# The seams of a spectral tower and its tail: conjugate spectra, loads ahead of barriers, 64 x 64 tiles in self attention, experts in double steps

## The chip, the core and the metric

The program runs on one core of one Trainium2 chip. The core has five engines with queues of their own: TensorE (PE in the rows; its weight loads are PEld), VectorE (DVE), ScalarE (ACT), GpSimd (POOL) and SyncE (SP), which here only issues DMAs. The engines meet at semaphores. The metric is device time in microseconds from the first to the last instruction of a run. Everything is computed in float32. In the rows one matmul of the program is two MATMUL entries, so "x4" under TensorE is two matmuls.

## What is computed

The kernel computes a vision tower (a spectral network of four layers with a head), and then two blocks of attention and mixture of experts on the tokens that it gives. Cut to what matters:

```
h = einsum('bhwi,ic->bhwc', x, fc0_w) + fc0_b                  # x: 64 images of 64 x 64 x 3, 64 channels
for l in range(4):
    xf = rfft2(h)                                              # 32 x 16 modes are kept
    of[top] = einsum('bixy,ioxy->boxy', xf[top], w1)           # a complex 64 x 64 product for each mode
    of[bot] = einsum('bixy,ioxy->boxy', xf[bot], w2)
    y = irfft2(of) + pw_w[l] @ h + pw_b[l]
    h = gelu(batchnorm(y))                                     # over all images and pixels
tok = gelu(h @ fc1_w + fc1_b) @ fc2_w + fc2_b                  # 4096 tokens of 64
h = tok
h = h + linear_attention(layernorm(h))                         # 4 heads of 32, softmax over q and over k
h = h + experts(layernorm(h))                                  # 8 experts, 64 -> 256 -> 64, top 2
h = h + self_attention(layernorm(h))                           # over the 64 rows of each image, masked rows
h = h + experts(layernorm(h))                                  # 16 experts, 64 -> 128 -> 64, top 2
```

## The kernel before

**Phases.** The tower is a row of phases. At the end of each, `phase_end` (L162) drains every engine and waits for all five. First comes `spectrum0`; then, for each of the four layers l, `mix` (the products of the modes) and `inverse` (the inverse transforms, the pointwise product, the sums for batch norm); after the inverse of layers 0 to 2 comes `forward` (batch norm, gelu and the forward transform of that layer's result), after the inverse of layer 3 the `head`. The tail has no barriers inside; there semaphores between engines order everything. All phases share one SBUF area, `arena`, and address it by offset. So a phase can load ahead of a barrier only into parts that the phase before has finished with.

**mix** (L305 to L392). The modes come in NCH = 8 chunks in three sets of buffers. SyncE loads a chunk of spectra (`spec_in`, 2 MB) and of weights (2 MB). The complex product is made as a real one of 128 rows: `s_sb[:, 0]` holds the real parts on the lower 64 partitions and the imaginary ones on the upper 64. `s_sb[:, 1]` is made from it by two copies: ScalarE copies the imaginary part up (L368), VectorE the real part down (L378), and then VectorE negates the imaginary part in place (L380, it waits for L368). TensorE (L356) waits for all three. A chunk's result is made in two parts v; each is turned by VectorE (L391) and stored to `spec_out` by SyncE (L321, 1 MB). The last thing SyncE does before the barrier is to wait until these stores have landed (L340).

**inverse** (L417 to L641). It goes over NP = 32 pairs of images p. The column transform `rows(p)` (L490) takes its operand from `grp`, the spectra of eight images, loaded by SyncE from `spec_out` in four DMAs of four modes for each group (L439). VectorE turns its result (L592) into the stationary operand `a2`. `columns(p, T)` (L514) multiplies that with `hin`, in which one half of the partitions holds a constant basis and the other the activations. The basis of `hin[0]` and of `hin[1]` is written by VectorE at the start of each inverse (`fill_basis`, L469, two copies each); TensorE's first `rows` waits for the first two. In layers 1 to 3 the activations come from `y_dram` in two halves (L445) through a gelu on ScalarE (L548); in layer 0 from the input, after VectorE has cleared four areas (L606). ScalarE takes the result out of PSUM (L557) and stores it to `y_dram` (L561, 2 MB for each p). VectorE gathers the sums for batch norm (L600). GpSimd writes the pointwise weights of the second `a2` (L474). At the end VectorE aggregates 32 x 8 sets of sums in one instruction (L621); a chain of small instructions follows on VectorE and TensorE, ScalarE takes the root (L577), but only once its stores have landed, and VectorE makes `scale` and `shift` (L634 to L638).

**forward and head.** Both begin with loads of `y_dram` (L665, L796, 2 MB each) into four buffers `hf`, which SyncE issues after the barrier, and with gelus of them on ScalarE (L733, L839).

**The tail** has TG = 8 groups of 512 tokens. `vector_norm` (L975) is nine VectorE instructions over all tokens with one root on ScalarE. TensorE then turns the normed tokens (L1050), and computes on. In `tensor_attention` TensorE's order for step n is project(n), context(n-1), attend(n-1), turn_k(n), project_out(n-1), turn_q(n). In `tensor_self` (L1560 to L1619) it is project(n) (q: L1568, v: L1570, k: L1571), turn_prob(n-1) (L1586), scores(n) (L1577), mix(n-1) (L1596), project_out(n-1) (L1603). Which part of the array a matmul uses follows from its shape: "64*64" in a row is 64 rows of the array by 64 columns, "128*64" all rows by 64 columns. In `tensor_experts` each of NST = 64 steps is a `hidden` (L1451, two matmuls of 512 columns, one on each half of the array's rows), a relu by ScalarE for even steps (L1507) and by VectorE for odd ones (L1542), and a `second` (L1460, two matmuls, one on each half of the array's columns). It runs in the order hidden(i), second(i-2). Once in eight steps come `bias` (L1466) and `turn_y` (L1474). VectorE also scales the inputs of the experts (L1523).

## Time and profile before

| | us |
|---|---|
| median of 3 runs | 4860.54 (4859.98 to 4867.24) |
| the profiled execution | 4854.42 |
| its span, first to last instruction | 4852.6 |

| engine | busy, us | share of the span |
|---|---|---|
| TensorE, matmuls | 3665.2 | 76% |
| VectorE | 2948.8 | 61% |
| ScalarE | 2495.9 | 51% |
| GpSimd | 55.2 | 1% |

The granted TensorE clock has a mean of 0.895 of 2.4 GHz. All times in the rows below are microseconds from the start of the span of that one execution. No single engine bounds the program: it is a row of stages, each with a limit of its own, and gaps between them.

### The profile page before, as it was taken

The page shows a single profiled execution, that of the slowest core. Times are in us where ns is not written, and L with a number is a line of the kernel's source. Part 1 is how long each engine was busy: PE and PEld are TensorE (multiplying, and loading weights), DVE is VectorE, ACT ScalarE, POOL GpSimd, SP SyncE. Part 2 cuts the span into 40 slices and gives each one's busy share as a digit, 9 for nine tenths or more (in the row PEclk, how much of TensorE's full clock was granted, in tenths as well). Part 3 has the DMA queues.
Part 4 walks back from the last instruction along what each step waited for, and adds up shares of the span by engine and source line. Part 5 has one row for each costly group of instructions (what it writes and reads, how often), then busy time and mean ns, then how long its engine had stood idle before and what let it go on. Part 6 is the DMA issues. An engine that isn't in the chain of part 4 may idle for free. (4 is left out here: it accounts for less than half of the span.)

```text
span 4852.6 us, 114628 instructions
## 1 busy us (share of the span) xinstructions
PE 3665.2 (76%) x50692; PEld 2490.2 (51%) x50692; DVE 2948.8 (61%) x3816; ACT 2495.9 (51%) x1895; POOL 55.2 (1%) x56
## 2 busy tenths in 40 slices
PE   5796995669777746687877566878886998669777
PEld 4475883447566634475666344656663222642432
DVE  1458997874677768845777688457773000543345
ACT  0112444432488854324889543248887998222221
POOL 0000000000000000000000000000000001000000
PEclk9898997889899978898999788989999999779578
DMA  1675776759688867596898676868886542011042
GB/s 36 246 296 181 253 254 247 291 213 362 237 336 340 324 245 287 221 354 241 337 340 331 247 275 227 334 245 334 331 334 236 201 176 99 1 36 36 1 88 62
DMA packets 213395, 1119.87 MB, mean 231 GB/s; under 512 B 24593, under 2 KB 96561, under 8 KB 138989
## 3 DMA queue, kind: packets, MB, share of 16 engines
q1 hardware_dynamic: 189390, 827.97, 46.7%
q10 hardware_dynamic: 22592, 285.22, 15.5%
q8 instruction: 297, 4.87, 0.4%
q0 software_dynamic: 1024, 1.05, 0.1%
q14 instruction: 92, 0.75, 0.0%
HBM read 709.04 MB, written 405.14 MB: 230 GB/s over the span
## 5 line engine op out<-in xcount | busy, mean ns | idle before, releaser
L514 PE MATMUL bank<-arena 128*64 128x128 f32 x16384 | 1137.5, 295 | 206.9 <-ACT arena L557 187.9
L514 PEld LDWEIGHTS bank<-arena 128*64 128x64 f32 x16384 | 1080.3, 221 | 360.0 <-issue 359.8
L548 ACT ACTIVATE arena<-arena,shift,scale 64x2048 f32<-64x2048 f32 x384 | 804.1, 2094 | 130.8 <-DMA arena<-y_dram 89.5
L600 DVE BATCH_NORM_STATS2 stats<-arena 128x6 f32<-128x512 f32 x1024 | 633.3, 671 | 299.6 <-ACT arena L557 299.5
L592 DVE STREAM_TRANSPOSE arena<-bank 64x512 f32<-64x512 f32 x1024 | 731.2, 714 | 68.5 <-PE bank L490 37.1
L557 ACT ACTIVATE arena<-bank,pwb 128x1024 f32<-128x1024 f32 x512 | 567.2, 1108 | 290.1 <-PE bank L514 282.3
L356 PE MATMUL bank<-arena 128*32 128x128 f32 x8192 | 589.7, 475 | 95.6 <-DVE arena L380 95.6
L733 ACT ACTIVATE arena<-arena,shift,scale 128x1024 f32<-128x1024 f32 x384 | 445.1, 1230 | 404.9 <-DMA arena<-y_dram 404.9
L693 PE MATMUL bank<-arena,fwq 32*32 32x512 f32 x6144 | 310.5, 825 | 354.6 <-DVE arena L739 354.6
L356 PEld LDWEIGHTS bank<-arena 128*32 128x32 f32 x8192 | 464.1, 134 | 221.0 <-issue 97.7
L739 DVE STREAM_TRANSPOSE arena<-arena 128x1024 f32<-128x1024 f32 x384 | 447.4, 1203 | 37.5 <-ACT arena L733 37.5
L490 PE MATMUL bank<-arena,ga 64*64 64x512 f32 x2048 | 288.8, 684 | 179.6 <-DMA arena<-spec_out 117.3
L710 PE MATMUL bank<-arena,ghq 32*32 32x256 f32 x12288 | 351.8, 426 | 20.6 <-issue 16.1
L368 ACT ACTIVATE arena<-arena 64x4096 f32<-64x4096 f32 x32 | 127.1, 3972 | 466.4 <-DMA arena<-spec_in 466.4
L693 PEld LDWEIGHTS bank<-arena,fwq 32*32 32x32 f32 x6144 | 98.0, 116 | 475.7 <-issue 466.6
L710 PEld LDWEIGHTS bank<-arena,ghq 32*32 32x32 f32 x12288 | 282.6, 111 | 108.0 <-issue 77.9
L391 DVE STREAM_TRANSPOSE arena<-bank 128x512 f32<-128x512 f32 x256 | 160.7, 687 | 287.2 <-PE bank L356 287.1
L744 DVE STREAM_TRANSPOSE arena<-bank 128x1024 f32<-128x1024 f32 x192 | 235.6, 1229 | 115.8 <-PE bank L693 115.8
L810 PE MATMUL bank<-arena,fc 64*128 64x512 f32 x1024 | 264.4, 624 | 14.6 <-ACT arena L839 13.1
L846 ACT ACTIVATE arena<-bank,fc1b 128x1024 f32<-128x1024 f32 x256 | 267.9, 1124 | 13.6 <-PE bank L810 13.6
L864 DVE TENSOR_SCALAR arena<-bank,fc2b 128x512 f32<-128x512 f32 x8 | 6.0, 752 | 404.8 <-PE bank L822 404.8
L490 PEld LDWEIGHTS bank<-arena,ga 64*64 64x64 f32 x2048 | 76.9, 145 | 285.3 <-issue 275.7
(195 smaller groups left out, 2537.6 us busy)
## 6 DMA issues: line engine op xcount, KB each, us to landing
y_dram<-arena ACTq DMA_DIRECT2D x128, 2048.0 KB, 7.9
arena<-y_dram SPq DMA_DIRECT2D x128, 2048.0 KB, 8.7
arena<-y_dram SPq DMA_DIRECT2D x192, 1024.0 KB, 7.3
arena<-spec_in SPq DMA_DIRECT2D x32, 2048.0 KB, 7.9
arena<-in_w_modes SPq DMA_DIRECT2D x32, 2048.0 KB, 13.8
spec_out<-arena SPq DMA_DIRECT2D x64, 1024.0 KB, 15.6
arena<-spec_out SPq DMA_DIRECT2D x128, 512.0 KB, 9.3
spec_in<-arena SPq DMA_DIRECT2D x24, 2048.0 KB, 13.9
```

Source lines behind the costliest of these rows:

```text
L356: mm = pe.matmul(bank[4 * v + k // 4][t * HB:(t + 1) * HB, k % 4 * 2 * B:(k % 4 + 1) * 2 * B], w_sb[u][:, mode, t // 2 * HB:(t // 2 + 1) * ...
L490: mm = pe.matmul(bank[2 * v + r][FREQ[par], :], ga[k_p, r * S:(r + 1) * S], grp[p // Q % 2][k_p, :, par * Q + q, :], start=True, stop=True ...
L514: mm = pe.matmul(hpx(bank[4 + T % 2 * 2 + j // 4][CHAN[par], :])[:, :, j % 4 * S:(j % 4 + 1) * S], a2[p % 2][par][:, :, rp], hpx(hin[u][pa ...
L548: act.activation(hpx(hin[u][par][CHAN[par]])[:, :, px], yin[v][CHAN[par]], ACT.Gelu, bias=shift[CHAN[par], :], scale=scale[CHAN[par], :]). ...
L557: act.activation(y, banks[:, 4 + T % 2 * 2:6 + T % 2 * 2, :].rearrange("p b (h x) -> p b h x", h=2), ACT.Identity, bias=pwb[:]).then_inc(y ...
L592: dve.transpose(a2[p % 2][par][FREQ[par], v * 32 + c0:v * 32 + c0 + 16, :], banks[FREQ[par], 2 * v:2 * v + 2, :].rearrange("p r (k c) -> p ...
L600: dve.bn_stats(stats[:, p * 48 + 6 * t:p * 48 + 6 * t + 6], by_half(yout[p % 2])[:, T // 2, h, T % 2 * BK:T % 2 * BK + BK]).then_inc(y_see ...
L693: mm = pe.matmul(bank[g][QUAD[c], :], fwq[QUAD[g], s * 32:(s + 1) * 32], hT[q % 2][QUAD[g], s, :, c * CQ:(c + 1) * CQ], start=(s == 0), st ...
L710: mm = pe.matmul(bank[4 + c][QUAD[j], 0:256], ghq[QUAD[c], col:col + K1], t1[q % 2][QUAD[c], v:4:2, hh, :, ri * M2:(ri + 1) * M2], start=( ...
L733: act.activation(x, x, ACT.Gelu, bias=shift[:], scale=scale[:]).then_inc(f_ready, 1)
L739: dve.transpose(hT[p % 2][:, :, row:row + 16, :].rearrange("p s h c -> p h s c"), hf[p % Q][:, v * 2 * BK:(v + 1) * 2 * BK].rearrange("p ( ...
L846: act.activation(gb[n % NB_G], banks[:, 2 * k:2 * k + 2, :].rearrange("p a b -> p (a b)"), ACT.Gelu, bias=fc1b[:]).then_inc(fc1_gelu, 1)
```

## The change

It has two parts. **In the tower:**
- The constants of both forward transforms are changed so that the stored spectrum is the complex conjugate. The imaginary half of the operand then already has the sign that L380 gave it. ScalarE's copy gets a factor of -1 and VectorE's negation goes.
- In mix, after the stores of chunk 6, SyncE waits until they have landed, then loads 14 of the 16 modes of the inverse's first group, and, in layers 1 to 3, both halves of the first pair's activations. Only then come the stores of the last chunk. The last two modes are loaded after the barrier. `yin`, `yout` and `hin` change places in the arena, so that these loads meet nothing that is in use.
- At the end of the inverse SyncE loads the first two of forward's or head's four buffers ahead of the barrier, once the columns of pair 30 are done.
- One of the four basis copies moves from VectorE to GpSimd, in front of GpSimd's two old copies; TensorE's first `rows` waits for it as for VectorE's.
- The aggregation for batch norm is made in four parts of eight pairs, three of them inside the loop; the end then combines four means and variances, with more small instructions.

**In the tail:**
- `vector_norm` works on two halves of the tokens, in the order centre(0), variance(0), centre(1), scale(0), variance(1), scale(1). The turns on TensorE wait for the first half only, and for the second from the fifth group on.
- In the linear attention project(n+1) runs ahead, between turn_k(n) and project_out(n-1); VectorE masks the context before it shifts the exponents.
- In self attention project(n+1) moves behind mix(n-1). q and k become two column tiles that read the same rows, v and the output projection are cut from four matmuls of 128 columns of the array to eight of 64. VectorE sums the exponents right after the shift, ahead of add_out.
- The experts run hidden(i), hidden(i+1), second(i-2), second(i-1).

```
-    part = np.stack([np.stack([cs, -sn], 1), np.stack([sn, cs], 1)], 0)
+    part = np.stack([np.stack([cs, sn], 1), np.stack([sn, -cs], 1)], 0)
...
+            def ahead():
+
+                for u in range(2):
+                    sp.wait_ge(mixed_stored[u], l * (NCH * 16) + (NCH * 16 + 32 - 32 * u))
+                    sp.sem_inc(waited[sp.engine], 1)
+                load_group(sp, l, 0, slice(0, M2 - 2))
+                if not first:
+                    for v in range(2):
+                        load_half(sp, l, 0, v)
 
...
+                if c == NCH - 2:
+                    ahead()
...
-                pe.wait_ge(imag_negated, n + 1)
...
-                act.activation(s_sb[u][0:C, 1], s_sb[u][C:P, 0], ACT.Copy).then_inc(imag_up, 1)
+                act.activation(s_sb[u][0:C, 1], s_sb[u][C:P, 0], ACT.Copy, scale=-1.0).then_inc(imag_up, 1)
...
                 dve.tensor_copy(s_sb[u][C:P, 1], s_sb[u][0:C, 0]).then_inc(real_down, 1)
-                dve.wait_ge(imag_up, l * NCH + (c + 1))
-                dve.tensor_scalar(s_sb[u][C:P, 0], s_sb[u][C:P, 0], -1.0, None, ALU.mult).then_inc(imag_negated, 1)
...
-        hin = [[at((2 * u + par) * PX, PX) for par in range(2)] for u in range(2)]
-        yout = [at((4 + u) * PX, PX) for u in range(2)]
-        yin = [at(6 * PX + v * PX // 2, 2, PX // 4) for v in range(2)]
+        hin = [[at((3 * u + par) * PX, PX) for par in range(2)] for u in range(2)]
+        yin = [at(2 * PX + v * PX // 2, 2, PX // 4) for v in range(2)]
+        yout = [at((5 + u) * PX, PX) for u in range(2)]
...
-            for i in range(Q):
-                load_group(0, i)
...
-                    load_group(p // Q + 1, p % Q)
...
+            sp.wait_ge(y_done, (l * NP + NP) * 4 + 4)
+            sp.sem_inc(waited[sp.engine], 1)
+            for q in range(2):
+                sp.dma_start(hf[q], y_dram[q]).then_inc(f_loaded[q], 16)
...
+            pool.tensor_copy(basis_of(0, 1), basis_from(1)).then_inc(filled[0], 1)
...
-            fill_basis(dve, 0)
+            dve.tensor_copy(basis_of(0, 0), basis_from(0)).then_inc(filled[0], 1)
             for i in range(8):
                 turn(0, i)
-            fill_basis(dve, 1)
+            for par in range(2):
+                dve.tensor_copy(basis_of(1, par), basis_from(par)).then_inc(filled[1], 1)
             for p in range(NP):
...
+                if p % 8 == 7:
+                    dve.wait_ge(y_seen, (l * NP + p) * 8 + 24)
+                    dve.sem_inc(waited[dve.engine], 1)
+                    dve.bn_aggr(part[:, p // 8, :], stats[:, (p - 7) * 48:(p + 1) * 48]).then_inc(bn_step, 1)
...
-            dve.bn_aggr(bn[:, 0:2], stats[:]).then_inc(bn_step, 1)
...
-                    load(lf * NG + g, g, q)
+                    if g > 0 or q > 1:
+                        load(lf * NG + g, g, q)
...
+            centre(0)
+            variance(0)
+            centre(1)
+            scale(0)
+            variance(1)
+            scale(1)
...
+                if g % (TG // 2) == 0:
+                    pe.wait_ge(x_ready, 2 * k + 1 + g // (TG // 2))
...
             pe.wait_ge(x_copied, TG)
+            project(0)
             for n in range(TG + 1):
-                if n < TG:
-                    project(n)
                 if n > 0:
                     context(n - 1)
                     attend(n - 1)
                 if n < TG:
                     turn_k(n)
+                if n + 1 < TG:
+                    project(n + 1)
                 if n > 0:
                     project_out(n - 1)
                 if n < TG:
...
                 if n < TG:
-                    shift(n)
+                    maxima(n)
                 if n > 0:
                     mask_context(n - 1)
                 if n < TG:
+                    shift(n)
                     sums(n)
...
-                    hidden(i)
+                    if i % 2 == 0:
+                        hidden(i)
+                        hidden(i + 1)
                 if i >= 2:
                     second(i - 2)
                     if (i - 2) % ST == ST - 1:
...
-                b0, b1, b2, b3 = lane_bank[g % 2]
+                u = g % 2
+                for j in range(2):
+                    pe.matmul(lane_bank[u][1][PAR[j], :], selfw[C:P, j * C:(j + 1) * C], xT2[C:P, g, :], start=True, stop=True,
+                              tile_position=(C, j * C))
                 if g > 1:
-                    pe.wait_ge(pT_copied, g - 1)
                     pe.wait_ge(oT_copied, 2 * g - 2)
-                    pe.wait_ge(so_taken, g - 1)
-                pe.matmul(b1[0:C, :], selfw[C:P, 0:C], xT2[C:P, g, :], start=True, stop=True)
                 for t in range(4):
-                    pe.matmul(b3[:, t * (C + 2):(t + 1) * (C + 2)], xT2[0:C, g, t * P:(t + 1) * P], selfw[0:C, 0:C + 2], start=True, stop=True)
-                pe.matmul(b2[0:C, :], selfw[C:P, C:2 * C], xT2[C:P, g, :], start=True, stop=True).then_inc(sproj_done, 1)
+                    for a in range(2):
+                        mm = pe.matmul(lane_bank[u][3][PAR[a], t * (C + 2):(t + 1) * (C + 2)], xT2[0:C, g, t * P + a * C:t * P + (a + 1) * C],
+                                       selfw[0:C, 0:C + 2], start=True, stop=True, tile_position=(0, a * C))
+                mm.then_inc(sproj_done, 1)
...
-                    mm = pe.matmul(lane_bank[u][3][:, t * C:(t + 1) * C], oT[u][:, t].rearrange("p a i -> p (a i)"), woT, start=True, stop=True)
+                    for a in range(2):
+                        mm = pe.matmul(lane_bank[u][2][PAR[a], t * C:(t + 1) * C], oT[u][:, t, a, :], woT, start=True, stop=True,
+                                       tile_position=(0, a * C))
                 mm.then_inc(so_done, 1)
...
             pe.wait_ge(x_copied, 3 * TG)
+            project(0)
             for n in range(TG + 1):
-                if n < TG:
-                    project(n)
                 if n > 0:
                     turn_prob(n - 1)
                 if n < TG:
                     scores(n)
                 if n > 0:
                     mix(n - 1)
+                if n + 1 < TG:
+                    project(n + 1)
+                if n > 0:
                     project_out(n - 1)
 
         def scalar_self(act):
...
+            values(0)
             for n in range(TG + 1):
                 if n < TG:
-                    values(n)
                     shift(n)
+                    sums(n)
+                if n + 1 < TG:
+                    values(n + 1)
                 if n > 0:
                     add_out(n - 1)
-                if n < TG:
-                    sums(n)```

TensorE in self attention, one step of the loop, first before. `L1568`, `L1570`, `L1571` are q, v and k of the projection, `L1586` turn_prob, `L1577` scores, `L1596` mix, `L1603` the output projection.

```order
L1568 MATMUL bank<-arena 64x512
L1570 MATMUL bank<-arena 128x66 x4
L1571 MATMUL bank<-arena 64x512
L1586 MATMUL bank<-ident,arena 64x64 x8
L1577 MATMUL bank<-arena 64x64 x8
L1596 MATMUL bank<-arena 64x64 x8
L1603 MATMUL bank<-arena 128x64 x4
```

And after: `L1660` is turn_prob, `L1649` scores, `L1670` mix, `L1635` q and k, `L1641` v, `L1678` the output projection.

```order
L1660 MATMUL bank<-ident,arena 64x64 x8
L1649 MATMUL bank<-arena 64x64 x8
L1670 MATMUL bank<-arena 64x64 x8
L1635 MATMUL bank<-arena 64x512 x2
L1641 MATMUL bank<-arena 64x66 x8
L1678 MATMUL bank<-arena 64x64 x8
```

The projection of the next group now stands between mix and the output projection, and no matmul writes 128 partitions any more.

TensorE in the experts, around one `turn_y` (`L1474`), before; `L1451` is hidden and `L1460` second.

```order
L1451 MATMUL bank<-arena 128x512 x2
L1460 MATMUL bank<-arena 64x512 x2
L1451 MATMUL bank<-arena 128x512 x2
L1460 MATMUL bank<-arena 64x512 x2
L1474 MATMUL bank<-arena 128x64 x4
L1451 MATMUL bank<-arena 128x512 x2
```

And after; `L1518` is hidden, `L1527` second, `L1541` turn_y, `L1533` bias.

```order
L1533 MATMUL bank<-arena 64x512
L1518 MATMUL bank<-arena 128x512 x4
L1527 MATMUL bank<-arena 64x512 x4
L1518 MATMUL bank<-arena 128x512 x4
L1527 MATMUL bank<-arena 64x512 x2
L1541 MATMUL bank<-arena 128x64 x4
L1527 MATMUL bank<-arena 64x512 x2
```

The two kinds alternate every two steps instead of every step, except around turn_y.

SyncE's queue at the end of mix in layers 1 to 3, before: `L321` stores the last chunk, `L166` is the barrier.

```order
L321 DMA spec_out<-arena 128x2048
L337 ISA
L340 REGISTER_ALU
L166 ISA
L439 DMA arena<-spec_out 128x4x256 x4
L445 DMA arena<-y_dram 128x2048 x2
L439 DMA arena<-spec_out 128x4x256
```

And after: `L326` is the wait of `ahead`, `L442` loads modes of the group, `L454` halves of the activations.

```order
L326 ISA
L326 REGISTER_ALU
L442 DMA arena<-spec_out 128x14x256
L454 DMA arena<-y_dram 128x2048 x2
L320 ISA
L321 DMA spec_out<-arena 128x2048
L320 REGISTER_ALU
L321 DMA spec_out<-arena 128x2048
L349 REGISTER_ALU
L166 ISA
L442 DMA arena<-spec_out 128x2x256
```

Two large loads now stand in front of both stores for which the barrier waits, and one small load is left behind it.

## Rows read from the trace of the kernel before

**Rows 1.** Stretches (us): PE, PEld, DVE, ACT, POOL busy, PEclk, DMA share, GB/s.
```profile
430.00:740.00 310.00, 298.30 (x4194) 255.52 (x4194) 302.75 (x465) 130.29 (x117) 0.00 (x0) 1.00 0.73 251
...
4516.00:4615.00 99.00, 82.27 (x544) 52.99 (x542) 23.47 (x80) 21.49 (x42) 0.00 (x0) 0.52 0.00 1
```

**Rows 2.** Timeline, start of mix, layer 1: start, us, engine, line [idle <-releaser].
```profile
1096.45 3.61 ACT L368 ACTIVATE arena<-arena 64x4096 f32<-64x4096 f32 x1 [48.10 <-DMA arena<-spec_in]
1096.57 2.29 DVE L378 COPY arena<-arena 64x4096 f32<-64x4096 f32 x1 [15.22 <-DMA arena<-spec_in]
...
1102.74 0.72 PE L356 MATMUL bank<-arena 128*32 128x128 f32 x5 [22.75 <-DVE arena L380]
```

**Rows 3.** Timeline, start of the inverse, layer 1.
```profile
1256.84 6.19 DVE L469 COPY arena<-fb 64x4096 f32<-64x4096 f32 x2 [4.16 <-SPq L165]
1256.86 7.92 POOL L474 COPY arena<-wst 64x2048 f32<-64x2048 f32 x2 [875.07 <-SPq L165]
...
1265.79 3.69 PE L490 MATMUL bank<-arena,ga 64*64 64x512 f32 x16 [15.68 <-DMA arena<-spec_out]
```

**Rows 4.** Timeline of GpSimd, start of the inverse, layer 0.
```profile
377.96 3.83 POOL L474 COPY arena<-wst 64x2048 f32<-64x2048 f32 x2 [376.84 <-SPq L165]
```

**Rows 5.** Timeline, end of the inverse of layer 0 and start of forward.
```profile
752.30 7.09 DVE L621 BATCH_NORM_AGGREGATE bn<-stats 128x2 f32<-128x1536 f32 x1
...
761.69 1.28 ACT L577 ACT_TABLE_LOAD   x1 [10.86 <-DVE bn L630]
...
772.62 4.63 ACT L733 ACTIVATE arena<-arena,shift,scale 128x1024 f32<-128x1024 f32 x4 [6.57 <-DMA arena<-y_dram]
777.52 4.64 ACT L733 ACTIVATE arena<-arena,shift,scale 128x1024 f32<-128x1024 f32 x4 [0.27 <-DMA arena<-y_dram]
```

**Rows 6.** Timeline, end of the inverse of layer 3.
```profile
3670.25 2.30 PE L514 MATMUL bank<-arena 128*64 128x128 f32 x32 [0.97 <-ACT arena L557]
...
3674.68 0.34 ACTq L561 DMA_DIRECT2D y_dram<-arena  x1
...
3694.74 1.28 ACT L577 ACT_TABLE_LOAD   x1 [10.84 <-DVE bn L630]
```

**Rows 7.** Timeline, steady experts, one step and the start of the next.
```profile
4344.81 1.13 PE L1451 MATMUL bank<-arena 64*128 64x512 f32 x4
...
4345.87 1.08 PE L1460 MATMUL bank<-arena 128*64 128x512 f32 x4
...
4346.88 1.13 PE L1451 MATMUL bank<-arena 64*128 64x512 f32 x4
```

**Rows 8.** Timeline of TensorE in the head: two pairs in a row, then the next kind.
```profile
3717.49 1.99 PE L810 MATMUL bank<-arena,fc 64*128 64x512 f32 x8
3719.41 1.06 PE L822 MATMUL bank<-arena 128*32 128x512 f32 x8
```

**Rows 9.** Timeline of self attention, one step of its loop.
```profile
4545.24 1.93 PE L1568 MATMUL bank<-arena 64*64 64x512 f32 x2 [0.60 <-DVE arena L1697]
...
4547.10 1.97 PE L1570 MATMUL bank<-arena 64*128 64x66 f32 x8
4549.00 1.97 PE L1571 MATMUL bank<-arena 64*64 64x512 f32 x2
4550.90 1.12 PE L1586 MATMUL bank<-ident,arena 128*64 128x64 f32 x16
...
4552.07 1.01 PE L1577 MATMUL bank<-arena 64*64 64x64 f32 x13
...
4552.93 1.10 PE L1596 MATMUL bank<-arena 64*64 64x64 f32 x15
...
4554.23 0.42 ACT L1628 ACTIVATE arena<-arena 128x256 f32<-128x256 f32 x1 [1.78 <-DVE arena L1681]
...
4555.23 1.97 PE L1603 MATMUL bank<-arena 64*128 64x64 f32 x8 [1.19 <-ACT arena L1643]
```

**Rows 10.** Timeline, the norm ahead of the first experts.
```profile
4285.20 2.29 DVE L978 TENSOR_REDUCE arena<-arena 128x32 f32<-128x2048 f32 x1
...
4298.19 2.19 PE L1050 MATMUL bank<-ident,arena 128*64 128x128 f32 x18 [28.51 <-DVE arena L1356]
```

**Rows 11.** By line: count, busy, mean ns, idle before and its releaser.
```profile
L1126 PE MATMUL bank<-arena 128*128 128x64 f32 x128 | 26.0, 388 | 16.9 <-DVE arena L1246 16.9
```

248 lines of the change are left out of this document (139 added, 109 removed).

## The prediction

> **What bounds the kernel now.** I read the by-stage windows first, to see which engine is full in which stage, and then the timeline at every place that the diff touches. There is no one bound. In the inverse of layer 0 VectorE is busy 302.75 of 310 us [rows 1], so what is added there to VectorE is paid in full. Self attention takes 99 us; TensorE is busy for 82.27 of them, at a granted clock of 0.52 [rows 1], in small matmuls. The experts are one matmul pair after another without a gap [rows 7]. At the seams of the tower TensorE stands still: mix starts with TensorE idle until the negation is done [rows 2], the inverse until the group of spectra has landed [rows 3], forward until `y_dram` has [rows 5]. Almost all edits aim at such places, so a time saved there ought to reach the end. What I had to ask of each is what comes second.
>
> **Self attention: 41 us off.** One step of the loop costs 99 / 8 = 12.4 us [rows 1]. TensorE's pieces are [rows 9]: q 1.86 (start to start), v 1.90, k 1.90, turn_prob 1.17, scores 0.86, mix 1.10, a wait of 1.19 for ScalarE's copy, output 1.97, a wait of 0.60. After the change q and k stand on two column halves of the array and share the stream, as `second` does in the experts, so they take one k, 1.9. v becomes eight matmuls in the form of scores, 66 columns for 64: 0.9 (at most what it took, 1.9). The output likewise: 0.9 (at most 1.97). Both waits have other work in front: copy_out runs while the projection does, and add_out is no longer waited for. That makes 1.17 + 0.86 + 1.10 + 1.9 + 0.9 + 0.9 = 6.8. Is the softmax next? It begins when scores end at 4553.2 (4552.07 and 1.1), its exp ends at 4554.65 [rows 9], and four short VectorE instructions follow (an estimate of 1.4, since the exp itself, on 256 elements, takes 0.42, and two of them are of that size): 3 us in all, against 1.1 + 1.9 + 0.9 + 0.9 = 4.8 of TensorE work that now stands between scores and turn_prob. So it is hidden, and the step is 6.7 to 6.8. Seven such steps are 47; the first (projection, copy, scores, softmax: 6) and the last (turn, copy, mix, copy, output, add: 5) add 11: 58 for 99, so 41 off. Bounds: 13 if no two tiles run side by side and only the waits go (a rival), 58 if the clock rises (another).
>
> **Experts: 20 us off.** A step is 2.07 us: hidden 1.06, second 1.01 [rows 7]. In the head two pairs of the form of hidden stand in a row and take 1.92 [rows 8]; so the second of two equal pairs costs 1.92 - 1.06 = 0.86, and a change of form costs 0.20. For second I take what 1.01 leaves above the same 0.86, 0.15. A double step is then 3.78 for 4.14. Of eight steps with bias and turn_y the old order has 17 changes of form and the new one 10 (turn_y splits a pair); 7 x 0.175 x 16 groups = 20. What would come next: relu. hidden(i+3) needs the relu of i+1, which on VectorE (about 1.2 us) begins when hidden(i+1) ends at 1.9 of 3.8 and is done at 3.2, 1.6 us before it is wanted. VectorE also scales one input a step in the second experts; it has some 1.1 us left in each double step. Range 8 to 23.
>
> **Norms: 10 us off.** The norm takes 4298.19 - 4285.20 = 13.0 us until TensorE may turn [rows 10]. It is five instructions of 2.29 and small ones. In halves (an estimate of 1.2 each, from the half of 2.29) the first half is ready after 1.2 x 6 and 7 small ones (2.3) = 9.7, the second after 14.4. TensorE needs over 5 us for the first half's turns, so it doesn't wait for the second. 3.3 us off for each of three norms; in the first norm only the last product gains (1.1), and the last norm, which nobody waits for in halves, loses 1.2. Range 5 to 12.
>
> **Linear attention: 4 us off.** TensorE waits 16.9 us in eight groups for the masked context [rows 11]. Masking earlier takes perhaps 0.7 of 2.1 us from each wait, and ScalarE's values now stand in front of copy_kT and give 0.2 back: 0.5 x 8. Range -3 (slower) to +8.
>
> **Start of mix: 10 us off.** TensorE starts at 1102.74 behind the negation. Without it, it starts behind ScalarE's copy, which ends at 1096.45 + 3.61 = 1100.06 [rows 2]; VectorE's own copy is done at 1098.9. 2.6 less for the way = 2.5, times four layers. The rest of mix is TensorE's, so nothing takes it back.
>
> **Mix to inverse: 9 us off.** Before, TensorE starts 8.95 us behind the barrier [rows 3], the load being last. Now only 256 KB are left to load; what is last are the basis copies. GpSimd's copy is new on the path: its two copies of 64x2048, together as large, took 3.83 in layer 0 [rows 4] and 7.92 in layer 1, where VectorE copied at the same time and took 6.19 for two copies [rows 3] that alone take 2.29 each [rows 2]. So the two engines hold each other up: 2.29 + 3.83 = 6.1 us until both are done. The start moves by 2.85. The Trainium skill has this as a rule: "SBUF — State Buffer", on engine ports and AXI ports, calls the port pair that VectorE and GpSimd share an exclusive lock, not a split of bandwidth. The trace agrees in size; by two copies side by side, without such a lock, the start would be at 3.9 and the three seams would give 6.6 us more. Against that stands SyncE: the loads ahead (3.8 MB) stand in front of the last two stores. At 4.9 us for 2 MB [rows 5] they take 9 to 11 us from about 1240, when chunk 6's stores have landed; the last store, issued at 1252.7, lands about 0.6 late, and the barrier with it. 2.2 x 3. In layer 0 one of two VectorE copies leaves the path, 2.3, and no activations are loaded ahead. Bounds 0 (the stores land 3 us late) to 16.
>
> **Inverse to forward and head: 30 us off.** ScalarE waits 6.57 us for `y_dram` behind its table load [rows 5]; with the loads ahead that goes, four times, if they have landed, which at 9.8 us for two they have. But they collide with the last stores, for whose landing ScalarE waits before its root. Layer 3: the loads start at 3669.3, when the columns of pair 30 end (those of pair 31 begin at 3670.25), the store of pair 30 at 3674.7, that of pair 31 at 3683.9 (3694.74 - 10.84) [rows 6]. 6 MB at 2 MB in 4.9 us are through at 3685.5, the last store at 3690.4. The batch norm chain without the large aggregation (7.09 [rows 5], now a quarter, 1.8, plus about 0.8 of small instructions) gives a root at 3690.3. So the root moves from 3694.7 to 3690.4, less 1 us that the three aggregations in the loop cost: 3.3 + 6.5 = 9.8 for each of layers 1 to 3. Layer 0 has no slack: its loop is VectorE's, so the three aggregations cost 3 x 1.9 = 5.7, and its last pairs follow each other so fast that 8 MB start within 9 us and end 19.6 later; the root comes 6 us late. 6.6 - 6.0 = 0.6. Bounds 12 to 38.
>
> **The sum.** 41 + 20 + 10 + 4 + 10 + 9 + 30 = 124. The profiled execution took 4854.4, so 4730; the median of the runs is 6.1 above it: 4737.
>
> **Rivals.**
> - **TensorE's clock rises in self attention.** It is 0.52 of 2.4 GHz there [rows 1], the 1.2 GHz level, while TensorE works 83% of the time with small parts of the array. The new step does the same in half the time. At the full clock TensorE's part is 3.4 and the softmax bounds the step at about 4.3: 7 x 2.5 = 17 less. 4720. Against it: the rows show the low level through nearly the whole stage at that busy share.
> - **The seams collide.** The loads ahead delay the stores for which root and barrier wait, in all layers as in layer 0: the terms of 9 and 30 shrink to 3 and 10. 4763. For it: 8 MB in 20 us is already all that the queues moved [rows 5].
> - **The tiles don't run side by side.** q and k then cost 1.86 and 1.90, v and the output 1.90 and 1.97 as before; the step is 10.8, and only 1.7 x 8 = 13 is left of the 41: 4765. Against it: the matmuls of scores, which have the new form, take 0.86 for eight where v takes 1.90 for four [rows 9].
> - **Slower than before.** One mechanism: in the experts' double step two hidden stand in front of both second, and if a relu is late, TensorE idles in each double step and its clock falls to the level of self attention. A double step then lasts 3.8 longer: 64 x 3.8 = 243, less the 104 of the other terms: 4998. It decides where relu is later than its 1.6 us of slack. Nothing in the rows points to it.
>
> **How the numbers follow.** The forecast has 0.6, the clock 0.12, the collisions 0.15, the tiles 0.1, slower 0.02, the rest 0.01. The bounds of the terms, taken as independent, are some 20 us either way, and the rivals within reach lie at 4720 to 4765; 4703 to 4780 leaves out about 2 in 10. A measurement of this kernel tells 0.2%, 9.7 us, from no change; all cases but the last are far beyond it: faster 0.96, same 0.015, slower 0.025.
>
> **What would show it.** Self attention: TensorE steps of 6.8 us, with turn_prob not waiting for VectorE. Experts: double steps of 3.8 without idle time. Mix: TensorE released by ScalarE's copy. Inverse: the first rows 6.1 us behind the barrier, released by GpSimd or VectorE; 3.9 would refute the lock, 9 the loads ahead. Forward: the first gelu right behind its table load. Root of layer 0 near 768, of layer 3 four microseconds earlier relative to the last sums. It is wrong above all if self attention isn't near 58 us, since that is a third of the sum.

## The result

The changed kernel takes 4731.5 us (median of 4 runs, 4728.9 to 4741.6), the kernel before 4860.3 in the same comparison (4859.2 to 4867.2): a ratio of 0.9736, with a 95% interval of 0.9719 to 0.9753. 124 us had been forecast on the profiled execution and 4737 on the median; the profiled execution of after has a span of 4729.0 us, 123.6 less than before. The sum is right, but that it came out to within 0.4 us is luck. Two terms were too high, by 8.5 and 5.7 us, and were made up for by gains of 5 and 6.4 that I had not seen. And the medians are 128.7 us apart, not 124.

To see where the time went I cut both traces at the same events, read from the timelines: the start of a stage's first instruction on its engine, and for a barrier the first instruction of any engine behind it. Times in us; "forecast" is the term of the prediction.

| stretch | before | after | difference | forecast |
|---|---|---|---|---|
| start of mix: copy to first matmul, four layers | 25.2 | 20.9 | -4.3 | -10 |
| mix to inverse: barrier to first rows, four layers | 50.5 | 38.5 | -12.0 | -9 with the next row |
| mix itself (the last stores land later), and ahead of it | | | +1.5 | |
| inverse, forward and head, four layers | | | -33.5 | -30 |
| linear attention, first turn to second norm | 137.7 | 142.2 | +4.5 | -4 |
| five norms (first instruction to first turn, or to the end) | 89.9 | 80.9 | -9.0 | -10 |
| gates, turn to first expert, two | 84.4 | 78.1 | -6.4 | none |
| experts, two stages | 308.0 | 289.7 | -18.3 | -20 |
| self attention, turn to next norm | 109.4 | 63.3 | -46.1 | -41 |

### The profile page after: what moved, and what is told of

Read it like the earlier page. It is cut to its first block and busy times, and to the rows that moved or that the text cites. A ratio compares the mean times of both kernels' runs of the same rounds, so it can differ in the third digit from the quotient of the medians.

```text
span 4729.0 us, 114991 instructions
## 1 busy us (share of the span) xinstructions
PE 3599.2 (76%) x50820; PEld 2529.5 (53%) x50820; DVE 2873.2 (61%) x3853; ACT 2498.1 (53%) x1908; POOL 64.6 (1%) x60
## 3 DMA queue, kind: packets, MB, share of 16 engines
q10 hardware_dynamic: 22592, 285.22, 15.9%
q0 software_dynamic: 1024, 1.05, 0.1%
## 5 line engine op out<-in xcount | busy, mean ns | idle before, releaser
L538 PE MATMUL bank<-arena 128*64 128x128 f32 x16384 | 1135.4, 295 | 205.2 <-ACT arena L582 186.0
L538 PEld LDWEIGHTS bank<-arena 128*64 128x64 f32 x16384 | 1078.6, 221 | 356.1 <-issue 355.9
L582 ACT ACTIVATE arena<-bank,pwb 128x1024 f32<-128x1024 f32 x512 | 567.3, 1108 | 302.1 <-PE bank L538 291.6
L367 PE MATMUL bank<-arena 128*32 128x128 f32 x8192 | 588.4, 474 | 90.8 <-DMA arena<-in_w_modes 90.8
L367 PEld LDWEIGHTS bank<-arena 128*32 128x32 f32 x8192 | 518.9, 136 | 160.3 <-issue 93.0
L772 DVE STREAM_TRANSPOSE arena<-arena 128x1024 f32<-128x1024 f32 x384 | 447.0, 1202 | 16.5 <-ACT arena L766 16.5
L514 PE MATMUL bank<-arena,ga 64*64 64x512 f32 x2048 | 285.2, 677 | 176.0 <-DMA arena<-spec_out 68.5
L379 ACT ACTIVATE arena<-arena 64x4096 f32<-64x4096 f32 x32 | 127.0, 3969 | 462.9 <-DMA arena<-spec_in 462.9
L743 PE MATMUL bank<-arena,ghq 32*32 32x256 f32 x12288 | 349.2, 424 | 18.9 <-issue 14.4
L843 PE MATMUL bank<-arena,fc 64*128 64x512 f32 x1024 | 264.7, 625 | 11.8 <-ACT arena L872 10.2
L514 PEld LDWEIGHTS bank<-arena,ga 64*64 64x64 f32 x2048 | 76.3, 144 | 280.7 <-issue 271.6
```

Of the source, the lines that this page charges most:

```text
L367: mm = pe.matmul(bank[4 * v + k // 4][t * HB:(t + 1) * HB, k % 4 * 2 * B:(k % 4 + 1) * 2 * B], w_sb[u][:, mode, t // 2 * HB:(t // 2 + 1) * ...
L514: mm = pe.matmul(bank[2 * v + r][FREQ[par], :], ga[k_p, r * S:(r + 1) * S], grp[p // Q % 2][k_p, :, par * Q + q, :], start=True, stop=True ...
L538: mm = pe.matmul(hpx(bank[4 + T % 2 * 2 + j // 4][CHAN[par], :])[:, :, j % 4 * S:(j % 4 + 1) * S], a2[p % 2][par][:, :, rp], hpx(hin[u][pa ...
L582: act.activation(y, banks[:, 4 + T % 2 * 2:6 + T % 2 * 2, :].rearrange("p b (h x) -> p b h x", h=2), ACT.Identity, bias=pwb[:]).then_inc(y ...
L743: mm = pe.matmul(bank[4 + c][QUAD[j], 0:256], ghq[QUAD[c], col:col + K1], t1[q % 2][QUAD[c], v:4:2, hh, :, ri * M2:(ri + 1) * M2], start=( ...
L772: dve.transpose(hT[p % 2][:, :, row:row + 16, :].rearrange("p s h c -> p h s c"), hf[p % Q][:, v * 2 * BK:(v + 1) * 2 * BK].rearrange("p ( ...
```

## The profile after

**Self attention.** By-stage window of after (columns as in [rows 1]), then one step of its loop.

```profile
4451.00:4503.00 52.00, 46.07 (x664) 35.01 (x656) 23.63 (x79) 22.67 (x50) 0.00 (x0) 0.54 0.01 2
```

```profile
4480.94 1.12 PE L1660 MATMUL bank<-ident,arena 128*64 128x64 f32 x16
4481.99 1.01 PE L1649 MATMUL bank<-arena 64*64 64x64 f32 x13
...
4482.85 0.84 PE L1670 MATMUL bank<-arena 64*64 64x64 f32 x11
4483.39 1.11 PE L1635 MATMUL bank<-arena 64*64 64x512 f32 x1
4483.43 0.42 PE L1670 MATMUL bank<-arena 64*64 64x64 f32 x3
...
4485.15 1.14 PE L1641 MATMUL bank<-arena 64*64 64x66 f32 x16
4486.08 1.06 PE L1678 MATMUL bank<-arena 64*64 64x64 f32 x16
4487.07 1.12 PE L1660 MATMUL bank<-ident,arena 128*64 128x64 f32 x16
```

Against [rows 9]: both waits are gone and the step is 6.13 us for 12.56. v (L1641) takes 0.93 for 1.90, the output (L1678) 0.99 for 1.97, q and k (L1635) 1.76 together for 1.86 and 1.90. The last matmuls of mix (L1670) stand beside the first of q and k, so that from the start of mix to that of q and k it is only 0.54 us. The granted clock is 0.54, as low as before.

**Experts.** Timeline of TensorE; L1518 is hidden, L1527 second.

```profile
4324.01 1.99 PE L1518 MATMUL bank<-arena 64*128 64x512 f32 x8
4325.93 1.94 PE L1527 MATMUL bank<-arena 128*64 128x512 f32 x8
4327.79 1.99 PE L1518 MATMUL bank<-arena 64*128 64x512 f32 x8
```

A double step is 3.78 us, as forecast from [rows 7, 8], and in both stages together TensorE waits once for a relu, for 0.4 us.

**Norm ahead of the first experts.** First instruction and first turn.

```profile
4240.90 1.22 DVE L1017 TENSOR_REDUCE arena<-arena 128x16 f32<-128x1024 f32 x1
...
4250.61 5.32 PE L1107 MATMUL bank<-ident,arena 128*64 128x128 f32 x64 [25.24 <-DVE arena L1421]
```

9.71 us where [rows 10] had 12.99; 9.7 was forecast.

**Start of mix, layer 1.**

```profile
1096.05 3.62 ACT L379 ACTIVATE arena<-arena 64x4096 f32<-64x4096 f32 x1 [48.83 <-DMA arena<-spec_in]
1096.17 2.29 DVE L389 COPY arena<-arena 64x4096 f32<-64x4096 f32 x1 [15.36 <-DMA arena<-spec_in]
...
1101.33 3.96 PE L367 MATMUL bank<-arena 128*32 128x128 f32 x52 [21.87 <-DMA arena<-in_w_modes]
```

TensorE's idle time ends with the landing of the weights, not with ScalarE's copy: it starts 5.28 us behind the start of that copy, for 6.29 in [rows 2].

**Start of the inverse**, layer 1, and GpSimd's copy in layer 0.

```profile
1256.27 2.29 DVE L632 COPY arena<-fb 64x4096 f32<-64x4096 f32 x1 [5.50 <-SPq L165]
1256.29 5.73 POOL L496 COPY arena<-fb 64x4096 f32<-64x4096 f32 x1 [872.71 <-SPq L165]
...
1262.36 3.69 PE L514 MATMUL bank<-arena,ga 64*64 64x512 f32 x16 [14.13 <-POOL arena L496]
```

```profile
376.20 3.59 POOL L496 COPY arena<-fb 64x4096 f32<-64x4096 f32 x1 [375.06 <-SPq L165]
```

In layers 1 to 3 the first rows start 6.1 us behind the barrier, released by GpSimd, as forecast. VectorE's copy takes its 2.29, and GpSimd's takes 5.73 beside it and 3.59 in layer 0, where VectorE clears an area at that time instead of copying: it is held up for 2.14 us, nearly as long as VectorE copied, and not by the clearing.

**End of the inverse**, layer 0 and layer 3 (compare [rows 5, 6]).

```profile
743.80 0.83 SPq L485 DMA_DIRECT2D arena<-y_dram  x2
...
751.93 1.12 ACT L582 ACTIVATE arena<-bank,pwb 128x1024 f32<-128x1024 f32 x1 [0.89 <-PE bank L538]
...
767.89 1.28 ACT L602 ACT_TABLE_LOAD   x1 [14.84 <-DMA y_dram<-arena]
```

```profile
3652.74 1.28 ACT L602 ACT_TABLE_LOAD   x1 [9.89 <-DMA y_dram<-arena]
...
3656.80 4.08 ACT L872 ACTIVATE arena<-arena,shift,scale 128x2048 f32<-128x2048 f32 x2
```

The root is released by the landing of the last store now, not by VectorE's chain, in every layer; the first gelu follows its table load without a gap. In layer 0 the root waits 14.84 us behind ScalarE's last copy where it waited 10.86.

**Linear attention**, one step. L1213 copies the values, L1228 kT; L1172 is context, L1181 attend.

```profile
4145.72 1.92 PE L1157 MATMUL bank<-ident,arena 128*68 128x128 f32 x8
...
4150.05 1.21 ACT L1213 ACTIVATE arena<-bank 64x512 f32<-64x512 f32 x2 [3.48 <-PE bank L1146]
...
4151.28 1.08 ACT L1228 ACTIVATE arena<-bank 68x512 f32<-68x512 f32 x2
...
4152.41 2.05 PE L1172 MATMUL bank<-arena 68*128 68x128 f32 x16 [0.94 <-ACT arena L1228]
...
4155.94 3.65 PE L1181 MATMUL bank<-arena 128*128 128x64 f32 x16 [1.47 <-DVE arena L1308]
```

The wait for the mask fell from 2.22 to 1.47, as forecast. A new one of 0.94 stands ahead of context: kT was turned at 4147.6, but its copy is queued on ScalarE behind the values of the projection that now runs ahead. The step stays at 13.66 us, and yet the stage is 4.5 us longer. Nearly all of that lies in the first step, from the first group's turn_k to the next one's: 16.92 us for 12.59. Its windows, after and before (columns as in [rows 1]):

```profile
4115.10:4132.00 16.90, 14.02 (x70) 12.27 (x71) 8.21 (x18) 3.56 (x6) 0.00 (x0) 0.50 0.00 1
```

```profile
4163.40:4176.00 12.60, 10.00 (x71) 8.48 (x72) 8.91 (x19) 3.44 (x6) 0.00 (x0) 0.77 0.01 1
```

The same matmuls ran at a granted clock of 0.50, where it was 0.77 before; the waits of the step differ by 0.2 us only.

## Experiments

All are edits of the changed kernel. The kernel before, measured on the same chip beside them, had medians of 4866.2 (la_old, la_kT, sa_wide, sa_order), 4871.9 in one run (w_halves, basis_act, aggr_end, no_pre), 4859.9 (seams2, ex_turn, best) and 4859.8 (la_mask). Totals of one run each were 4751.1 (sa_wide), 4752.1 (sa_order), 4724.4 (w_halves), 4745.5 (basis_act), 4754.6 (aggr_end), 4743.6 (no_pre), 4714.2 (seams2) and 4739.2 (ex_turn). Single executions of one kernel differ by 10 to 18 us, those of the kernel before by up to 33, so I compare stretches of the traces, and use the total only for the last kernel. Each edit has one trace. The total of aggr_end shows why: it lies far above the 6 us either way that were expected, and 9.4 us of that stand in the linear attention, whose code it didn't touch. Nine traces (after and eight edits that leave the ends of inverse alone) serve as a base for the tower. In layers 1 to 3 they have 466.8 us from first rows to root on average (463.3 to 469.9, 27 values; before, three values: 469.8). In layer 0 they have 371.6 (371.2 to 372.3; before 361.5).

### Self attention: form or order

```
sa_wide:
-                    for a in range(2):
-                        mm = pe.matmul(lane_bank[u][3][PAR[a], ...], xT2[0:C, g, t * P + a * C:...], ..., tile_position=(0, a * C))
+                    mm = pe.matmul(lane_bank[u][3][:, ...], xT2[0:C, g, t * P:(t + 1) * P], ...)
(the output projection likewise)
sa_order, TensorE:
-            project(0)
             for n in range(TG + 1):
+                if n < TG:
+                    project(n)
...
-                if n + 1 < TG:
-                    project(n + 1)
(copy_qk, values, sums and add_out in their old places too)
```

> The changed kernel with v and the output projection of self attention cut as before, four matmuls of 128 columns of the array each in place of eight of 64; the new order of the loop and the two column tiles of q and k stay. Theory: the narrow form is what saves: v goes from 0.93 to 1.90, the output from 0.99 to 1.97, the step from 6.13 to 8.1 us, self attention from 53 to 68, the kernel from 4731 to 4746. Rival: the order saved most, since these matmuls stand where TensorE would wait for the softmax anyway: the step grows by under 1 us and the kernel by under 8.

> The changed kernel with the old order of the self attention loop on TensorE, ScalarE and VectorE (project(n) at the head of the step, sums behind add_out), the new column tiles kept. Theory: the order is worth the two waits of before, 1.19 and 0.60 us, plus the softmax, which then has only turn_prob, mix and the projection in front of it: the step goes from 6.13 to between 7.9 and 9 us, the kernel to between 4743 and 4751. Rival: the tiles did it all, and the step stays within 0.5 us of 6.13: 4731 to 4735.

Timeline of sa_wide, v (L1640) and output (L1676) at the low level of the clock and, one step later, at the full one; then of sa_order, one step from output to output.

```profile
4488.02 1.97 PE L1640 MATMUL bank<-arena 64*128 64x66 f32 x8
4489.79 1.91 PE L1676 MATMUL bank<-arena 64*128 64x64 f32 x8
...
4495.83 1.10 PE L1640 MATMUL bank<-arena 64*128 64x66 f32 x8
4496.77 1.05 PE L1676 MATMUL bank<-arena 64*128 64x64 f32 x8
```

```profile
4492.22 0.80 PE L1678 MATMUL bank<-arena 64*64 64x64 f32 x10 [1.19 <-ACT arena L1720]
4492.72 1.12 PE L1635 MATMUL bank<-arena 64*64 64x512 f32 x2
...
4493.13 0.76 PE L1641 MATMUL bank<-arena 64*64 64x66 f32 x10
...
4495.15 1.13 PE L1660 MATMUL bank<-ident,arena 128*64 128x64 f32 x16 [0.47 <-DVE arena L1769]
...
4499.37 0.80 PE L1678 MATMUL bank<-arena 64*64 64x64 f32 x10 [1.19 <-ACT arena L1720]
```

sa_wide: a step is 8.10 us at the low level (turn_prob at 4469.86 and 4477.96), as expected, but from then on every second step runs in part at the full clock (0.71 over the step, 0.56 over the next), and two steps take 13.66. The stretch from turn to next norm grows by 6.8 us, not by 15. sa_order: the step is 7.15, and both waits are back (1.19 and 0.47). So the old order costs 1.0 us a step, less than I expected, and the stretch grows to 71.1. It costs less than its waits of 1.66, because in that order q and k (L1635) and v (L1641) start while the output projection (L1678) is still running. So the 6.4 us that a step has lost don't split into independent parts: undoing the order alone costs 1.0, undoing the form of v and output 2.0, q and k by the rows are another 2.0 and were undone by no kernel, and 1.4 are left to the edits together. In the wide form the clock rose in places; in the eleven traces with the narrow form and the new order all inner steps take 6.06 to 6.14 us.

### Linear attention

```
la_old:  project(n), values(n) and shift(n) back in their old places on TensorE, ScalarE and VectorE
la_mask: as la_old, but mask_context(n - 1) stays ahead of shift(n)
la_kT, ScalarE:
             for n in range(TG + 1):
-                if n > 0:
-                    copy_kT(n - 1)
                 if n < TG:
                     exps(n)
                 if n > 0:
                     copy_att(n - 1)
+                if n < TG:
+                    copy_kT(n)
                 if n + 1 < TG:
                     values(n + 1)
```

> The changed kernel with the linear attention alone put back: project(n) at the head of the step, VectorE masks the context behind the shift, ScalarE copies the values behind copy_kT. Theory: the change made this stage slower, 142.2 us from the first turn on TensorE to the next norm where it was 137.7, because the copy of kT now stands behind the values on ScalarE (0.94 us of wait in each step) and turn_q of the first group stands behind a second projection. Then the stage goes back to 137.7 and the kernel loses 4.5 us: 4727. Rival: only TensorE's granted clock differed by chance in the first steps (0.60 against 0.77 in the first 15 us), and the order has no part in it: the stage stays at 142 and the time at 4731.

> The changed kernel with one swap on ScalarE in the linear attention: copy_kT(n) is queued ahead of values(n+1). Theory: the kT of a group is ready 3.6 us before its copy starts, the copy waits behind the values of the projection that now runs ahead; with the swap the wait of 0.94 us ahead of the context matmuls goes in each of seven steps, the step falls from 13.66 to 12.7 and the kernel to 4724 or 4725. Rival: another engine's chain (VectorE's shift and sums, then turn_q) sets the step at 13.66, and the wait only moves: 4731.

> The changed kernel with the order of TensorE and ScalarE in the linear attention put back (project(n) at the head of the step), but VectorE's mask kept ahead of the shift: the part of the edit that my prediction counted. Theory: the projection that runs ahead is what made the stage slower, and the mask alone gives the 0.75 us of shorter wait in each step: the stage takes 138.15 - 8 x 0.75 = 132 from the first turn to the next norm, 10 less than in the changed kernel. Rival: the granted clock alternates between its levels in this stage and sets the step whatever the waits are: 138 to 142.

Attend (L1181) in la_kT, two steps from start to start, and in la_mask, one; and a window of la_mask over such steps.

```profile
4150.35 2.74 PE L1181 MATMUL bank<-arena 128*128 128x64 f32 x16 [1.48 <-DVE arena L1308]
4161.65 3.65 PE L1181 MATMUL bank<-arena 128*128 128x64 f32 x16 [1.48 <-DVE arena L1308]
4174.56 3.02 PE L1181 MATMUL bank<-arena 128*128 128x64 f32 x16 [1.48 <-DVE arena L1308]
```

```profile
4179.01 3.65 PE L1181 MATMUL bank<-arena 128*128 128x64 f32 x16 [1.47 <-DVE arena L1305]
4195.91 3.65 PE L1181 MATMUL bank<-arena 128*128 128x64 f32 x16 [1.47 <-DVE arena L1305]
```

```profile
4170.00:4225.00 55.00, 49.61 (x250) 45.53 (x250) 23.85 (x48) 12.47 (x21) 0.00 (x0) 0.50 0.00 1
```

| kernel | linear attention | gate behind it | sum |
|---|---|---|---|
| before | 137.7 | 41.1 | 178.8 |
| la_old | 138.2 | 41.1 | 179.2 |
| after | 142.2 | 35.5 | 177.7 |
| eight edits elsewhere | 142.0 to 142.4 (six), 148.3, 151.6 | 34.9 to 35.7 | 177 to 187 |
| la_kT | 131.5 | 35.4 | 166.8 |
| la_mask | 146.8 | 38.2 | 185.0 |

la_old agrees with its number for the stage: 138.2, 4 us less than after. Of the two causes that I gave, the wait of 0.94 isn't one: the inner steps are 13.66 us, as in after. The 4 us are in the first step (12.54 for 16.92), the one in which turn_q stands behind a second projection, and there it is the granted clock that differs. But the gate grows by 5.5 and takes the gain back. la_kT takes away the wait of 0.94: its inner steps take 11.3 and 12.9 us, and the stage 131.5. How much of that is the wait isn't shown: best, below, has the same order here and took 141.4. la_mask refutes my theory. The wait is as short as it should be (1.48), the first steps take 11.3 to 12.9, but then three take 16.3 to 16.9, with TensorE busy for 49.61 of 55 us at a granted clock of 0.50. The rival was right in kind, but I gave it too narrow a range: between 131 and 152 us the stage's time depends on how many of its steps run at the low level (16.9 us), at both in turn (13.66) or mostly at the full one. The totals don't separate these kernels: 4731.5 for after, 4734.0 (la_kT), 4742.6 (la_old) and 4738.4 (la_mask), medians of 4, with 12 to 18 us between the runs of one kernel. In the first step the level goes with the order: it was 0.50 in all eleven kernels in which project(1) stands ahead of the first turn_q (steps of 16.9 us, 15.2 in la_kT and best), and 0.77 in the three in which it doesn't (12.1 to 12.6). Why, and what decides in the later steps, these runs don't show.

The gate is the same effect. In before and la_old a group of matmuls of the gate takes 1.05 us at first and 1.87 from 10 to 12 us after TensorE's restart on; in after and la_kT none takes more than 1.09. TensorE's pause ahead of it was 25.2 us in both la_old and after, so the length of the pause doesn't decide. Nor does the stage before it by itself: in ex_turn the second gate fell to the low level as well (0.50 over 8 us where after has 0.81 at the same place), behind a self attention with the code and the time of after. The cause stays open. These 5.6 us were in no term of mine.

### Start of mix

```
w_halves:
-                sp.dma_start(w_sb[u], d["w_modes"][l, c]).then_inc(w_loaded[u], 16)
+                for v in range(2):
+                    sp.dma_start(w_sb[u][:, v * K1:(v + 1) * K1], d["w_modes"][l, c][:, v * K1:(v + 1) * K1]).then_inc(w_loaded[u][v], 16)
...
                 for v in range(2):
+                    pe.wait_ge(w_loaded[u][v], third(l, c))
```

> The changed kernel with each 2 MB load of mix's weights in two halves of 1 MB, each with a semaphore of its own; TensorE waits for the second only ahead of the second half of the modes. Theory: the start of mix no longer hangs on the copies but on the landing of the first weights, 5.3 us behind the landing of the first spectrum, where ScalarE's copy takes 3.6: with the first half landed at about 2.7 us TensorE starts 4.1 to 4.3 us behind it, 1.0 to 1.2 earlier in each of four layers, 4 to 5 us in all: 4727. Rival: the halves are moved by all queues together and land together: TensorE still starts at 5.3, 4731; or smaller packets slow all later loads: over 4733.

```profile
1092.79 3.62 ACT L380 ACTIVATE arena<-arena 64x4096 f32<-64x4096 f32 x1 [48.72 <-DMA arena<-spec_in]
...
1096.86 3.61 PE L368 MATMUL bank<-arena 128*32 128x128 f32 x45 [20.51 <-ACT arena L380]
```

TensorE starts 4.07 us behind the start of the copy and is released by its end: 1.2 us less in each of three layers and 1.3 in layer 0, 5.0 in all. This is the start that I had forecast for the change itself. The landing of the weights was what came second.

### Start of the inverse

```
basis_act:
-            pool.tensor_copy(basis_of(0, 1), basis_from(1)).then_inc(filled[0], 1)
...
+            act.activation(basis_of(0, 1), basis_from(1), ACT.Copy).then_inc(filled[0], 1)
seams2, further: ScalarE's two copies of wst count on a2_filled, for which TensorE waits ahead of columns(0, 0)
```

> The changed kernel with the basis copy that the change gave to GpSimd given to ScalarE, ahead of its two copies of the pointwise weights. Theory: GpSimd stands still while VectorE copies (5.73 us in layers 1 to 3, where VectorE copies for 2.29 of them, and 3.59 in layer 0, where VectorE does not); ScalarE does not share that: its copy takes about 3.6 beside VectorE's 2.29, and TensorE's first rows start 4.0 to 4.3 us behind the barrier in place of 6.1, unless the last 256 KB land later. GpSimd's own copies of the pointwise weights then take about 3.84 plus up to 2.29. Three times 2.0 less, 4725; in layer 0 nothing. Rival: ScalarE is held up as GpSimd is, or the last load lands at 6: 4731.

Timelines of seams2, layer 1.

```profile
1249.91 3.62 ACT L593 ACTIVATE arena<-fb 64x4096 f32<-64x4096 f32 x1 [50.86 <-SPq L165]
1249.93 2.29 DVE L638 COPY arena<-fb 64x4096 f32<-64x4096 f32 x1 [5.29 <-SPq L165]
1249.95 5.97 POOL L501 COPY arena<-wst 64x2048 f32<-64x2048 f32 x2 [872.06 <-SPq L165]
...
1253.86 2.84 PE L517 MATMUL bank<-arena,ga 64*64 64x512 f32 x12 [11.79 <-ACT arena L593]
```

ScalarE's copy takes 3.62 us beside VectorE's, as it does in layer 0 beside a clearing, while GpSimd's two copies of the weights stretch from 3.83 [rows 4] to 5.97. basis_act itself came out slower than after at this place (first rows 7.7 us behind the barrier), because I had overlooked that TensorE's wait also counts ScalarE's two copies of `wst`, which now end later; with a semaphore for each, in seams2, the start is 3.95 us behind the barrier. So a copy on VectorE and one on GpSimd hold each other up (in [rows 3] VectorE's own two took 6.19 for 4.58), and ScalarE neither of them. The Trainium skill states it so ("SBUF — State Buffer", on who interferes with whom): a VectorE instruction of certain kinds, a copy among them, or a GpSimd instruction takes the ports that the two share for its whole length, and ScalarE waits for nobody. These rows agree: GpSimd takes 2.1 us longer beside a copy of 2.29.

### End of the inverse

```
aggr_end: the four bn_aggr of a layer together, behind the loop over p
no_pre:
-            for q in range(2):
-                sp.dma_start(hf[q], y_dram[q]).then_inc(f_loaded[q], 16)
(forward and head load all four behind the barrier)
seams2:
-            for q in range(2):
-                sp.dma_start(hf[q], y_dram[q]).then_inc(f_loaded[q], 16)
+            sp.dma_start(hf[0], y_dram[0]).then_inc(f_loaded[0], 16)
+            for u in range(2):
+                sp.wait_ge(y_stored[u], l * (NG * 32) + (NG * 32 + 16))
+            sp.sem_inc(waited[sp.engine], 1)
+            sp.dma_start(hf[1], y_dram[1]).then_inc(f_loaded[1], 16)
```

> The changed kernel with the four quarter aggregations of the batch norm together at the end of the inverse, in all layers, instead of three of them in the loop. Theory: in layer 0, where the loop is VectorE's, the three cost 5.7 us in the loop, and the root waits there for the landing of the last stores anyway: from the first rows to the root 371.6 us fall to about 366. In layers 1 to 3 the chain behind the last sums grows by 3 x 1.9 = 5.7, minus what the landing of the last store hides (the root waits for it now): the root comes 1 to 4 us later there. In all between 6 us faster and 6 slower. Rival: in layer 0 the delay is the loads ahead and not the aggregations: the 371.6 stay.

> The changed kernel without the loads ahead of the barrier at the end of the inverse: forward and head load all four buffers behind it. Theory: each first gelu waits 6.5 us again behind its table load, in four layers, 26 us more; against it the last stores land earlier, and the root with them, by 1 us in layers 1 to 3 and by 4 to 6 in layer 0: 4731 + 26 - 8 = 4749. Rival: the loads ahead delay the stores by as much as they save, and the gain came from the aggregation: within 5 us of 4731.

> The changed kernel with two edits at different places. (1) ScalarE makes the second basis copy, ahead of its copies of the pointwise weights, which now have a semaphore of their own that TensorE waits for ahead of the first columns, not ahead of the first rows. Theory: beside VectorE's copy ScalarE's takes 3.62, its time alone, so the first rows start 4.1 us behind the barrier in layers 1 to 3 where it was 6.1: 6 us in all. Rival: the last 256 KB land later than that, and the start stays at 5 to 6. (2) Only one of forward's buffers is loaded ahead of the last stores, the second behind their landing. Theory: without loads ahead the root comes 3.6 us earlier in layers 1 to 3 and 7.7 in layer 0; it is the 4 MB in front of the stores that hold them up. With 2 MB ahead the root of layers 1 to 3 comes within 1 us of the kernel without loads ahead (462 to 466 from the first rows), that of layer 0 at 366 to 368, and the first gelu still starts right behind its table load: 2 to 3 us in each of three layers, 4 in layer 0, 10 to 13 in all. Rival: the second buffer, loaded behind the landing, is late by up to 6 us for the third gelu and takes it all back. Sum by theory: 16 to 19 us faster than the changed kernel on the same chip.

Timeline of no_pre, the root of layer 0 and the first gelu of forward; then of seams2, the same.

```profile
759.14 1.28 ACT L598 ACT_TABLE_LOAD   x1 [6.48 <-DMA y_dram<-arena]
...
762.21 1.28 ACT L761 ACT_TABLE_LOAD   x1 [1.58 <-DVEq L165]
...
769.92 4.63 ACT L761 ACTIVATE arena<-arena,shift,scale 128x1024 f32<-128x1024 f32 x4 [6.43 <-DMA arena<-y_dram]
```

```profile
760.62 1.28 ACT L608 ACT_TABLE_LOAD   x1 [9.98 <-DMA y_dram<-arena]
...
763.69 1.28 ACT L772 ACT_TABLE_LOAD   x1 [1.58 <-DVEq L165]
764.99 5.77 ACT L772 ACTIVATE arena<-arena,shift,scale 128x1024 f32<-128x1024 f32 x5
```

| first rows to root | layer 0 | layers 1 to 3 (mean) | root to next copy, L0, L1, L2; to the tail |
|---|---|---|---|
| before | 361.5 | 469.8 | 334.8, 337.5, 341.7; 428.5 |
| base of nine, after among them | 371.6 | 466.8 | 328.4, 332.5, 331.3; 421.9 |
| aggr_end | 365.4 | 469.8 | 330.8, 331.5, 334.7; 421.8 |
| no_pre | 363.9 | 463.5 | 335.3, 338.4, 337.6; 428.0 |
| seams2 | 366.5 | 461.9 | 329.0, 334.0, 334.1; 422.1 |

Down the columns this takes the seam apart. The aggregations in the loop cost layer 0 6.2 us (371.6 against 365.4) and bring the others 3.0. The two loads ahead save 6 to 7 us behind each root, but make the root 7.7 us later in layer 0 (371.6 against 363.9) and 3.3 later in the others. So in layer 0 they lose 0.8 us on balance and in layers 1 to 3 they win about 3 each. That is 7.8 in all; no_pre lies 2.8 us outside the range of the nine traces, which is 12 us wide over the same stretches. Where the tail begins no_pre is 7 us behind kernels with the tower of after (4087.7 against 4080.7, the mean of seven), not the 18 that I expected. One load ahead and one behind the landing keeps nearly both: the root is as early as without loads, in layer 0 to 2.6 us, and no gelu waits for a load. 1.5 and 2.8 us are lost again behind the roots of layers 1 and 2, but not the rival's way: the third gelu isn't late. What grows is ScalarE's gap ahead of the first table load behind the barrier, 7.12 and 7.45 us for 5.15 and 4.40 in after; the profile names nothing that it waits for, so the cause is open. At the start of the tail seams2 is 22 us ahead (4058.3), 14.8 by the ends of the inverse and 6.5 by its starts; 16 to 19 were expected for its two edits.

The wait behind ScalarE's last copy splits the root of layers 1 to 3 further. It was 10.84 us before, is 6.53 in no_pre, where the chain and the landing of the last store (6.3 us behind the copy) end together (4.3 less, the forecast had 4.4), 7.6 to 10.6 in the base, where the stores set it, and 11.7 in aggr_end. The loop up to that copy got 2 us shorter (459.0 to 457.0 in no_pre), not 1 longer.

### Experts, and all together

```
ex_turn:
-                if S_ == 4 and G > 0:
+                if S_ == 5 and G > 0:
                     turn_y(G - 1)
best: w_halves, la_kT, seams2 and ex_turn, and in layer 0 the four bn_aggr behind the loop
```

> The changed kernel with turn_y in the experts one step later, behind both matmul pairs of second instead of between them. Theory: a change of form costs 0.15 to 0.20 us, and here one of two changes goes in each of 14 groups: 14 x 0.15 to 0.2 = 2 to 3 us off, each expert stage 143.3 in place of 144.4 and 145.3. Rival: the price is one of waiting, not of form (turn_y and the copy of the sum hold each other up): the stages stay, or grow because the copy of the next sum comes late.

> All edits together that gained in single runs or should: the weights of mix in halves (4 to 5 us), copy_kT ahead of the values (10.7 in the linear attention), basis copy on ScalarE with a semaphore of its own (6), one load ahead and one behind the landing (10), the aggregations of layer 0 at its end (6, part of which the landing of the stores may take), turn_y one step later (2). They lie at different places of the program and should add up to 35 to 40: 4692 to 4697. Rival: those at the seams share one limit, the DMA queues, and half of their gain goes: about 4707.

ex_turn: the expert stages take 143.3 and 144.0 us for 144.4 and 145.3, 2.4 in all, as priced: a change of form costs 0.15 to 0.2. (Its total, 4739.2 in one run, holds a second gate of 48.6 us where after has 42.5; that is the clock, as said above, and not the edit.) best takes 4710.4 us (median of 5, 4707.4 to 4717.3), a ratio of 0.9694 to the kernel before (0.9681 to 0.9707), 21 us or 0.4% less than after, measured at another time. That is little more than half of what the single edits promised, so the rival came nearer. Its profile is of the slowest of the five runs. In it the start of mix (4.07 us) and of the inverse (3.95 behind the barrier) are as in the single runs, and the root of layer 0 (362.0) is 9.6 earlier than in the base. What is missing is 4 and 6 us behind the roots of layers 1 and 2 (336.5 and 337.8 to the next copy) and the linear attention: 141.4 us where la_kT had 131.5, with two steps of 15.9 and 16.1, and 41.8 in the gate. So the rival's number came nearer, but its reason, a limit that the seams share, isn't what most of the loss shows: 16 us of it are the granted clock in the linear attention and the gate.

## Why the prediction was right, and where it wasn't

**Self attention** (forecast 41, measured 46). The mechanism and its pieces held: 0.93 and 0.99 for v and output (0.9 forecast), 1.76 for q and k (1.9). What was mis-sized is mix, 0.54 us from start to start for the 1.10 that I took from [rows 9]: there a wait stood behind mix, here its last matmuls run beside the first of q and k.

**Experts** (20, measured 18.3) and **norms** (10, measured 9.0) held with their working; ex_turn confirms the price of a change of form.

**Linear attention** (4 faster, measured 4.5 slower). The failed step is "ScalarE's values now stand in front of copy_kT and give 0.2 back". They give back 0.94, so that with the 0.75 from the mask the step stayed at 13.66. That alone makes no loss. The 4.5 us are in the first step, where the granted clock was 0.50 for 0.77, and for which the sum had no term. The sum by waits doesn't bound this stage at all, since its steps follow the granted clock (la_mask). The same clock gave back 5.6 us in the gate behind it, unforeseen.

**Start of mix** (10, measured 4.3). The failed step is "TensorE starts behind ScalarE's copy". I asked what comes second among the engines and left out the weights' load; w_halves shows that the copy bound was right for the case without it (4.07 us measured, 3.8 forecast).

**Mix to inverse** (9, measured 10.5 with the later barriers). The 1.5 us more are mostly layer 3, where the first rows had started 10.2 us behind the barrier and not 8.95 as in layer 1. 6.1 us, the release by GpSimd and the late stores (mix in layers 1 to 3 longer by 0.2 to 0.9, 0.6 forecast) are all there. The price of 3.9 without the lock, named there as what would refute it, is to be had with ScalarE (seams2, 3.95).

**Inverse to forward and head** (30, measured 33.5 in the profiled execution; against the base of nine 27, from 22 to 34, so that the profiled one is a lucky draw). The right sum hides two mis-sized terms. In layer 0 the root came at 767.89, "near 768", yet since the layer's first rows began 3.9 us earlier that is 10.1 late and not 6: the aggregations' 6.1 and the stores' 4.0 add up, where I had let the longer stand for both. In layers 1 to 3 the root moved by 3.0 on average for 3.3, but not by my working: chain and loop would have brought 6.3 (no_pre), and the stores took 3.3 back. I had the last one land 6.5 us behind ScalarE's last copy, just as the chain ends; it landed 7.3 to 10.3 behind it. The rival "the seams collide" was half right, and its half is what seams2 takes back.

**Slips in the working.** The norm's pieces add up to 9.5 and not 9.7, and the three transfers of 4.9 us from 3669.3 on end at 3684.0 and not 3685.5; neither moves the sum by 1 us.

**Rivals.** The clock did not rise in self attention (0.54). The tiles do run side by side (sa_wide). In the experts one relu is late, by 0.4 us.

## What to carry over

A load issued ahead of a barrier is not free: ask which store is still to land, and put in front of it only what is needed first; two 2 MB loads ahead gained 7.8 us here over none, and one ahead with one behind the landing another 14.8. When an edit takes away the last release of a wait, list the transfers among the candidates for what comes second, not the engines alone. And where the granted clock changes within a stage, a shorter wait is no shorter time: compare such a stage over several kernels before believing a gain of a few per cent.

## What I had not expected of the hardware

- In the steps of the linear attention TensorE's granted clock changes between its two levels, 1.2 and 2.4 GHz, while no wait is longer than 1.5 us; it was at the low one over 55 us in which TensorE was busy for 49.6. The same stage of the same code took 142.0 to 151.6 us in nine kernels. Its first step ran at 0.50 in the eleven kernels that have one order of its matmuls, and at 0.77 in the three that have the other.
- The gate's matmuls slow down from 1.05 to 1.87 us 10 to 12 us after a restart, or don't, behind the same pause of 25.2 us. The cause is open.
- GpSimd's copy of 64x4096 takes 3.59 us beside a VectorE clearing and 5.73 beside a VectorE copy of 2.29 that isn't slowed; ScalarE's takes 3.62 in both cases.
- Two 2 MB loads in front of the last 2 MB stores delay their landing: the last store landed 6.3 us behind ScalarE's last copy in no_pre, 7.3 to 10.3 behind it with the loads in layers 1 to 3, and 14.4 to 15.3 in layer 0.
